# Edge streams of a four-part graph network: one-hots, scores and weights moved between VectorE, ScalarE and PSUM

## The reference

```python
score = f(table[src], dst_row[dst])          # layers 1 and 2: leaky_relu(xl[src] + xr[dst] + edge_attr @ We.T) @ att
smax  = segment_max(score, dst)
es    = exp(score - smax[dst])
alpha = es / segment_sum(es, dst)
out   = segment_sum(alpha * message[src], dst)
```

## Time and profile before

| | |
|---|---|
| median of 3 runs | 13644.97 us (13634.25 to 13649.05) |
| the profiled execution | 13576.47 us, its span 13574.4 us |
| TensorE, products | busy 10504.2 us (77%) |
| TensorE, weight loads | 8732.6 us (64%) |
| VectorE | 8519.3 us (63%), 15,786 instructions |
| ScalarE | 2406.7 us (18%) |
| GpSimd | 9220.1 us (68%) |
| DMA | 912.63 MB, mean 67 GB/s |

### The profile page before, as it was taken

One profiled execution on the slowest core, in us unless ns is written; L12 is line 12 of the kernel. 1 busy time (PEld: TensorE's weight loads), 2 busy tenths in 40 slices (PEclk: granted clock), 3 DMA queues, 4 the chain that ended last, 5 costly groups with the idle time before them and its releaser, 6 DMA issues. The chain is left out here.

```text
span 13574.4 us, 346433 instructions
## 1 busy us (share of the span) xinstructions
PE 10504.2 (77%) x102671; PEld 8732.6 (64%) x102672; DVE 8519.3 (63%) x15786; ACT 2406.7 (18%) x4954; POOL 9220.1 (68%) x8386
## 2 busy tenths in 40 slices
PE   2388888857888888488888857888888578888872
PEld 1377777746777777377777735777777357777762
DVE  7567777755777777355555544777777446666664
ACT  0011212111111122022222211111111112222220
POOL 0177777756777776577777735777777257777761
PEclk9855556555555555555555555555555555555555
DMA  0333333323333332222222223232222233333320
GB/s 16 84 75 71 73 73 73 73 42 75 72 72 73 73 71 57 39 55 54 55 54 55 54 54 106 77 78 77 77 78 72 69 96 78 78 78 78 78 64 11
DMA packets 771899, 912.63 MB, mean 67 GB/s; under 512 B 400125, under 2 KB 447616, under 8 KB 769760
## 3 DMA queue, kind: packets, MB, share of 16 engines
q0 software_dynamic: 267232, 390.16, 15.0%
q1 hardware_dynamic: 503008, 498.92, 13.0%
HBM read 791.99 MB, written 96.35 MB: 65 GB/s over the span
## 5 line engine op out<-in xcount | busy, mean ns | idle before, releaser
L914 POOL DMA_INDIRECT bs_gat<-table_b,bs_idx x1568 | 1750.7, 1117 | 506.5 <-issue 477.5
L914 POOL DMA_INDIRECT ds_gat<-table_d,ds_idx x1568 | 1749.3, 1116 | 506.7 <-issue 506.7
L914 POOL DMA_INDIRECT as_gat<-table_a,as_idx x1568 | 1740.9, 1110 | 506.6 <-issue 477.5
L914 POOL DMA_INDIRECT es_gat<-table_e,es_idx x1568 | 1725.7, 1101 | 505.6 <-issue 505.6
L914 POOL DMA_INDIRECT cs_gat<-table_c,cs_idx x1568 | 1731.0, 1104 | 491.0 <-issue 491.0
L1174 PE MATMUL ds_psM<-dstW_d,ds_hot 128*128 x9408 | 1252.7, 232 | 194.4 <-DVEq L1107 72.2
L1174 PE MATMUL es_psM<-dstW_e,es_hot 128*128 x9408 | 1253.5, 226 | 175.9 <-issue 65.3
L1174 PE MATMUL cs_psM<-dstW_c,cs_hot 128*128 x9408 | 1232.0, 183 | 182.3 <-DVEq L1100 68.9
L1174 PEld LDWEIGHTS ds_psM<-dstW_d,ds_hot 128*128 128x128 bf16 x9408 | 972.2, 103 | 481.6 <-issue 241.1
L1174 PEld LDWEIGHTS es_psM<-dstW_e,es_hot 128*128 128x128 bf16 x9408 | 962.6, 102 | 480.8 <-issue 224.4
L1174 PEld LDWEIGHTS cs_psM<-dstW_c,cs_hot 128*128 128x128 bf16 x9408 | 967.5, 103 | 473.0 <-issue 223.3
(11 more groups left out here) (758 smaller groups left out, 17937.2 us busy)
## 6 DMA issues: line engine op xcount, KB each, us to landing
as_rank<-rel_d SPq DMA_DIRECT2D x196, 256.0 KB
as_ea<-in_eaT SPq DMA_DIRECT2D x196, 256.0 KB
bs_rank<-rel_d SPq DMA_DIRECT2D x196, 256.0 KB
bs_ea<-in_eaT SPq DMA_DIRECT2D x196, 256.0 KB
cs_rank<-rel_d SPq DMA_DIRECT2D x196, 256.0 KB, 3.2
ds_rank<-rel_d SPq DMA_DIRECT2D x196, 256.0 KB, 3.3
es_rank<-rel_d SPq DMA_DIRECT2D x196, 256.0 KB, 3.4
table_e<-et_st SPq DMA_DIRECT2D x49, 544.0 KB, 2.7
```

Of the source, the lines that this page charges most:

```text
L914: g_.indirect_dma_start(gat[s][:, j, :], None, table, bass.IndirectOffsetOnAxis(ap=idxS[s][:, j:j + 1].bitcast(U32), axis=0)).then_inc(got ...
```

## The change

1. `hot` is made by ScalarE: `Square(rank - p)` into a new tile `off`, then `Relu(1 - off)`, each for two halves of 1,024 elements. Four activations stand at the end of ScalarE's step in place of two compares at the beginning of VectorE's.
2. `ahot` is laid out tile by tile. Eight `tensor_scalar` compare an iota row of 256 fp32 in a PSUM bank (`psI`) with one column of `m["rel"]` (now fp32). `psI` takes the bank of `psY`, whose parts move into `psX`.
3. In a, b, c and e `wtd` and `res` are one PSUM tile `psW`. Weigh writes it, rest subtracts in place, low reads it. Weigh waits for the low of the group before.
4. In a and b the score works in place on `psM`. ScalarE writes a fifth of the sum to `act`, VectorE waits for it and takes the maximum. `took` is given behind the reduce.
5. TensorE's transposes wait for `alphad` where they waited for `lowered`, as `psX` holds more.

```diff
-        ahot = [sb(f"ahot{s}", [P, 2 * P, GROUP], BF16) for s in range(2)]
-        mid = [sb(f"mid{s}", [P, GROUP, D]) for s in range(2)]
+        off = sb("off", [P, 2, GE], BF16)
+        ahot = [sb(f"ahot{s}", [P, GROUP, 2 * P], BF16) for s in range(2)]
...
-        psX, psY = ps("psX"), ps("psY")
+        psX, psI = ps("psX"), ps("psI")
+        if i != 3:
+            psW = ps("psW", 1024)[:, 0:GROUP * CW].rearrange("p (j c) -> p j c", c=CW)
+            wtd, res = [psW, psW], [psW, psW]
...
             def _(a):
...
+                def onehot(it, s):
+
+                    g = it * RING + s
+                    a.wait_ge(fed[s % 4], it * (3 * FEED) + (s // 4) * FEED + FEED)
+                    wait(a, made, g - 1)
+                    wait(a, hots, g)
+                    for x in range(2):
+                        a.activation(off[:, x, :], rank[s % 4][:, :], ACT.Square, bias=m["pidN"][:, x:x + 1]).then_inc(apart, 1)
+                    for x in range(2):
+                        a.wait_ge(apart, g * 2 + (x + 1))
+                        last = a.activation(hot[s % 2][:, x, :], off[:, x, :], ACT.Relu, bias=m["one"][:, 0:1], scale=-1.0)
+                    last.then_inc(hots, 1)
...
+                    if i <= 1 and within(u, GROUPS):
+                        a.wait_ge(added, u + 1)
+                        a.activation(act[s % 2][:, :, :].rearrange("p j f -> p (j f)"), psM[s % 2][:, :], ACT.Copy, scale=0.2).then_inc(fifth, 1)
...
+                    if within(u + 2, GROUPS):
+                        if known(u):
+                            onehot((u + 2) // RING, (u + 2) % RING)
+                        else:
+                            onehot(it if s + 2 < RING else it + 1, (s + 2) % RING)
...
             def _(v):
...
+                v.tensor_copy(psI[:, 0:2 * P], m["iota"][:, :]).then_inc(xch, 1)
...
-                def onehot(it, s):
-                    g = it * RING + s
-                    v.wait_ge(fed[s % 4], it * (3 * FEED) + (s // 4) * FEED + FEED)
-                    wait(v, made, g - 1)
-                    for a in range(2):
-                        last = v.tensor_scalar(hot[s % 2][:, a, :], rank[s % 4][:, :], m["pid"][:, a:a + 1], None, ALU.is_equal)
-                    last.then_inc(hots, 1)
...
                 def weigh(k, ks, kc):
                     v.wait_ge(alphad, kc + 1)
+                    if i != 3:
+                        wait(v, low, k)
...
                 def collect_hot(k, ks):
                     wait(v, summed, k * 2 - 2)
-                    v.tensor_tensor(ahot[ks % 2][:, :, :], over(m["rel"][:, bass.ds(k * GROUP, GROUP)], 1, [P, 2 * P, GROUP]),
-                                    m["rankX"][:, :, :], ALU.is_equal).then_inc(ahots, 1)
+                    for j in range(GROUP):
+                        last = v.tensor_scalar(ahot[ks % 2][:, j, :], psI[:, 0:2 * P], m["rel"][:, bass.ds(k * GROUP + j, 1)], None, ALU.is_equal)
+                    last.then_inc(ahots, 1)
...
                     if i <= 1:
-                        y = act[s % 2]
-                        link(v.tensor_tensor(x[:, :, :], dst3, gat[s][:, :, 0:D], ALU.add))
+                        link(v.tensor_tensor(dst3, dst3, gat[s][:, :, 0:D], ALU.add))
+                        v.sem_inc(added, 1)
+                        v.wait_ge(fifth, g + 1)
+                        link(v.tensor_tensor(dst3, dst3, act[s % 2][:, :, :], ALU.max))
+                        link(v.tensor_tensor(dst3, dst3, over(m["vec"][:, VECS.index(f"att{i + 1}"), :], 1, [P, GROUP, D]), ALU.mult))
+                        v.tensor_reduce(sc[s // CG][:, 0, q:q + GROUP], dst3, AX_X, ALU.add).then_inc(scored, 1)
+                        v.wait_ge(scored, g + 1)
                         v.sem_inc(took, 1)
-                        link(v.scalar_tensor_tensor(y[:, :, :], x[:, :, :], 0.2, x[:, :, :], ALU.mult, ALU.max))
-                        link(v.tensor_tensor(x[:, :, :], y[:, :, :], over(m["vec"][:, VECS.index(f"att{i + 1}"), :], 1, [P, GROUP, D]), ALU.mult))
-                        v.tensor_reduce(sc[s // CG][:, 0, q:q + GROUP], x[:, :, :], AX_X, ALU.add).then_inc(scored, 1)
...
-                                    last = pe.matmul(sums[h][a][:, bass.ds(w, 1), :], ahot[ks % 2][:, a * P:(a + 1) * P, j],
+                                    last = pe.matmul(sums[h][a][:, bass.ds(w, 1), :], ahot[ks % 2][:, j, a * P:(a + 1) * P],
...
                     if r == 0 and live:
                         pe.wait_ge(scored, xc * CG + CG)
-                        wait(pe, lowered, xc)
+                        wait(pe, alphad, xc)
```

More of the change, by code:

```diff
@@ L154, in build @@
             ident=sb("ident", [P, P]),
-            rankX=sb("rankX", [P, 2 * P, GROUP], BF16),
-            pid=sb("pid", [P, 2]),
+            iota=sb("iota", [P, 2 * P]),
+            pidN=sb("pidN", [P, 2]), one=sb("one", [P, 1]),
             vec=sb("vec", [P, len(VECS), D]),
@@ L265, in prepare @@
         LOADS = 10
-        MADE = 22
+        MADE = 23
         with nc.Block() as block:
@@ L328, in _ @@
                        allow_small_or_imprecise_dtypes=True).then_inc(made, 1)
-                g.iota(m["pid"][:, :], pattern=[[P, 2]], base=0, channel_multiplier=1,
+                g.memset(m["one"][:, :], 1.0).then_inc(made, 1)
+                g.iota(m["pidN"][:, :], pattern=[[-P, 2]], base=0, channel_multiplier=-1,
                        allow_small_or_imprecise_dtypes=True).then_inc(made, 1)
@@ L818, in stream @@
         else:
+            mid = [sb(f"mid{s}", [P, GROUP, D]) for s in range(2)]
             red = [sb(f"red{s}", [P, GROUP, 4]) for s in range(2)]
@@ L834, in stream @@
             tk1 = sb("tkO", [1, 2, P])
-        wtd = [sb(f"wtd{s}", [P, GROUP, CW]) for s in range(2)]
-        res = [sb(f"res{s}", [P, GROUP, CW]) for s in range(2)]
+        if i == 3:
+            wtd = [sb(f"wtd{s}", [P, GROUP, CW]) for s in range(2)]
+            res = [sb(f"res{s}", [P, GROUP, CW]) for s in range(2)]
         parts = [sb(f"parts{s}", [P, 3, GROUP, CW], BF16) for s in range(3)]
@@ L848, in stream @@
         masked = [sem(f"masked{s}") for s in range(3)]
-        hots, made, took, scored, sch, xch, ready, blank, wl, pch, sub, past = (
-            sem(n) for n in ("hots", "made", "took", "scored", "sch", "xch", "ready", "blank", "wl", "pch", "sub", "past"))
+        hots, made, took, scored, sch, xch, ready, blank, wl, pch, sub, past, apart, added, fifth = (
+            sem(n) for n in ("hots", "made", "took", "scored", "sch", "xch", "ready", "blank", "wl", "pch", "sub", "past", "apart", "added", "fifth"))
         turned, ended, gaveE, carried, gaveC, lowered, exped, backed, alphad = (
@@ L931, in step @@
                         a.wait_ge(backed, xc + 1)
-                        a.activation(alpha[xs][:, :, :].rearrange("p h t -> p (h t)"), psY[:, 384:384 + R], ACT.Copy).then_inc(alphad, 1)
+                        a.activation(alpha[xs][:, :, :].rearrange("p h t -> p (h t)"), psX[:, 256:256 + R], ACT.Copy).then_inc(alphad, 1)
                     if within(k, GROUPS):
@@ L941, in step @@
                         a.activation(Ex[:, :], Dx[:, :], ACT.Exp, scale=spec["scale"]).then_inc(exped, 1)
+                    if i <= 1 and within(u, GROUPS):
+                        a.wait_ge(added, u + 1)
+                        a.activation(act[s % 2][:, :, :].rearrange("p j f -> p (j f)"), psM[s % 2][:, :], ACT.Copy, scale=0.2).then_inc(fifth, 1)
                     if i == 3 and r == 3 and within(xc, CHUNKS):
                         a.wait_ge(backed, xc + 1)
-                        a.activation(alpha[xs][:, 0, :], psY[:, 384:384 + CT], ACT.Copy).then_inc(alphad, 1)
+                        a.activation(alpha[xs][:, 0, :], psX[:, 256:256 + CT], ACT.Copy).then_inc(alphad, 1)
+                    if within(u + 2, GROUPS):
[3 more added lines that the diff above has]
+                            onehot(it if s + 2 < RING else it + 1, (s + 2) % RING)
+                onehot(0, 0)
+                onehot(0, 1)
                 rounds(a, step, END)
@@ L993, in neighbours @@
                     return take.rearrange("a (x n) -> a x n", x=2)[:, :, 0:R - 1]
-                given = psY[0:1, 0:2 * (P + 1)].rearrange("a (x n) -> a x n", x=2)[:, :, 0:R - 1]
+                given = psX[0:1, P:P + 2 * (P + 1)].rearrange("a (x n) -> a x n", x=2)[:, :, 0:R - 1]
                 def highest(xc, xs, xq):
@@ L1195, in give_ends @@
                     pe.sem_inc(past, 1)
-                    pe.transpose(psY[0:1, 0:R], ends[:, 1:2], m["ident"][0:R, 0:R])
-                    pe.transpose(psY[0:1, P:P + R], ends[:, 0:1], m["ident"][0:R, 0:R]).then_inc(sem_out, 1)
+                    pe.transpose(psX[0:1, P:P + R], ends[:, 1:2], m["ident"][0:R, 0:R])
+                    pe.transpose(psX[0:1, 2 * P:2 * P + R], ends[:, 0:1], m["ident"][0:R, 0:R]).then_inc(sem_out, 1)
                 def give_carry(sem_in, value, sem_out):
@@ L1202, in give_carry @@
                     for x in range(2):
```

(4 more changed lines are left out.)

22 lines of the change are left out of this document (7 added, 15 removed).

## The result

The changed kernel takes 14,315.2 us (median; 14,307.5 to 14,316.4), the kernel before 13,647.0 us on the same chip: ratio 1.049, 95% interval 1.047 to 1.051. The forecast was 14,250 us, in a range of 13,850 to 14,900 us. The profiled execution spans 14,312.0 us, 738 us more than before's 13,574.4 us.

A forecast was written before the change was run, and what follows sets the result against it. Gathers set the pace at 11.3 us a group, TensorE next at 10.9. Layers a and b +257 us each, d +133, c and e -16 each: +615 us, about 14,190, plus 68; said 14,250 us, range 13,850 to 14,900 us.

The forecast's parts named there:

- VectorE's added work: VectorE, layers a and b: one-hots +1.23 us a group, weigh's wait +0.12, wait for ScalarE's copy +0.73, late `took` +0.81.
- reduce to flush: Score's end in a and b: `took` comes after the reduce, so 0.69 + 1.13 = 1.82 us, +0.81 us a group.
- the wait for the copy: Score in a and b: VectorE waits after the add for ScalarE's 512-element copy, 0.89 us, +0.73 us a group.
- low to weigh: VectorE, all layers but d: weigh waits for low, which breaks an overlap, +0.12 us a group (none to 0.23).
- 9.75 us a group in a without the gathers: VectorE's need in layer a before the change: 11.33 less 1.58 us waiting for gathers, its TensorE waits still included.
- Late one-hots in a, b and d: Expansion one-hots from ScalarE coming late: no term in a and b, an estimated 0.2 us a group in d.
- ScalarE's chain from flush to one-hots: ScalarE, each step: one-hot pair ready 11.1 us after the flush, leaving 1.3 us in hand before TensorE's next expansion.
- 10.93 - 0.2: TensorE's own need a group in c and e, less 0.2 us for the contiguous `ahot`; 0.47 us of lateness added, 11.20.
- Rival 3: ScalarE's chain holds TensorE in every step: +700 us, 14,950 us; decides from 0.3 us an op on; chance 0.08.
- Rival 1: Compares cheap (0.26 us each, 2.1 in all), gathers' gain kept: -160 us, 13,490 us; decides below about 0.28 us; chance 0.12.
- The rest of the span does not change: Outside the five streams: tables, merges and finishes were taken to stay as before, adding nothing to the sum.
- The 68 us between profile and median: Kernel before: median 13645.0 us against 13576.5 us profiled; this gap was added to about 14,190 us, giving 14,260 us.

## Why the prediction was right

The direction and the size came out, and part of the mechanism. The streams of a and b were forecast at 2,465 us and took 2,438 and 2,441, d's at 2,350 and took 2,370, c's and e's at 2,185 and took 2,234 and 2,245. But in a, b and d two terms of the sum were wrong, one too high and one too low. That they cancelled to 0.1 us a group was luck.

- *VectorE's added work.* Each term was close: compares 3.14 us (3.16 forecast), reduce to flush 1.81 us (1.82), the wait for the copy +0.56 us (+0.73), low to weigh +0.18 us (+0.12).
- *The base under them failed.* I took "9.75 us a group in a without the gathers" and wrote that the waits for TensorE were still in it, but did not take them out. These rows of the kernel before, waits in layer a, are what was left in:
```profile
DVE as_A L1001 <- PE as_psX L1226: 68.0, 39, 3.9
...
DVE as_carry L1018 <- PE as_psY L1203: 33.4, 35, 3.2
...
DVE as_accS L966 <- PE as_psA L1189: 27.3, 47, 1.0
```
They are 129 us, 0.66 us a group. With the terms as measured, 9.75 - 0.66 + 1.21 + 0.18 + 0.56 + 0.80 = 11.84 us (1.21 is 3.14 - 1.14 - 0.79), near the 11.81 us of the run with VectorE's one-hots. My 12.64 us were 0.83 too high. In d I had 11.85 us and that run gives 11.09. There the subtraction alone doesn't do it: the waits for TensorE in d of before are 242 us, 1.24 us a group, and 10.62 - 1.24 + 1.23 = 10.61 us is too low. Why stays open.
- *Late one-hots in a, b and d failed too.* I gave them 0, 0 and 0.2 us; they cost 0.69, 0.7 and 1.07. I had costed ScalarE's chain from flush to one-hots in an ordinary step. There it fits: in b the flushes of after stand 10.96 and 11.33 us apart, VectorE's own need of about 11. The chunk steps stand 13.42 and 13.59 us apart. In the run with VectorE's one-hots they stand 12.72 and 13.46 us apart (in layer a), 11.93 and 12.67 less the 0.79. By the rows of b what holds them is the wait of ScalarE for `added`, behind which the one-hots are queued; no usable run took out that wait alone. I costed that queue for the exponential in c and e, and did not see that the same engine order puts it behind the new copy in a and b.
- *c and e.* The late one-hots were forecast at 0.47 us a group and cost 0.46 and 0.50 (11.46 and 11.51 against 11.00 and 11.01); TensorE's wait in the chunk step is 2.13 us (1.9). The streams still got longer, since TensorE's own need is 11.0 us a group and not 10.93 - 0.2. The products did get faster (3.13 to 2.90 us in c). By how much my 10.93 was too low, and in which of TensorE's pauses, stays open.
- *Rival 3* was the truth for 0.7 to 1.1 us a group, by the chunk steps (in d, two of four steps have waits of 2.7 to 3.3 us) and not, as I priced it, by a dearer operation. Its point of decision was misplaced: ScalarE's operations are 1.04 us apart, as forecast (1.03).
- *Rival 1* was right in half: the gathers did get shorter, and eight compares that write `ahot` contiguously win 2% once they read the bf16 row and nothing waits. How much of that comes from shorter gathers and how much from faster products no run separates.
- *"The rest of the span does not change"* missed 51 us. At the end of a stream only sums are left. Their step was 4.63 us in c, with 0.64 us of it a wait for TensorE, and is 6.37 us with VectorE alone to set it. From the last score to the last sum each of the five streams now takes 11 to 12 us longer.
- The 68 us between profile and median that I carried over were before's alone; after has 1 us. In spans the forecast was +615 us against +738.

The undone parts don't price the change fully: what the score's stalls cost beside the other two costs was to be read from the two runs that fell into TensorE's pauses, and is only argued from its rows (1.36 us a group on VectorE). Shown is their price without the others, 0.4 us a group.

## What to carry to other kernels

Work that is moved to an engine with spare time goes behind that engine's waits. Follow it in the step in which those waits are longest, not in the mean step, and put it ahead of them where its inputs allow. When you estimate the need of an engine without its present bound, take out its waits for everyone (in a that came out to 0.03 us, in d it took out too much), and check that undoing one cost does not only lengthen the wait at another: here two edits gave 1.0% and 0.65% alone and 5.5% together.

## What the runs showed of the hardware

- A `tensor_scalar` compare of 256 elements with a pointer scalar starts 0.39 us after the one before when it reads fp32 from PSUM and 0.20 us after it when it reads bf16 from SBUF (eight in 3.14 and 1.63 us). The Trainium skill, "VectorE: DVE Perf Modes" (Why PSUM operands drop a tier), caps a PSUM source in fp32 at the basic rate; the slower compares from PSUM are in line with it. No run here reads fp32 from SBUF or bf16 from PSUM, so place and type of the source are not told apart.
- With the SBUF source and all else as changed a gather in a takes 986 ns on average, with the PSUM source 955, and in the kernel before, with its operation on two SBUF sources, 1,110. With that one operation replaced by the eight compares from SBUF it is 1,054.
- An activation of 1,024 bf16 elements with a pointer bias takes 1,138 ns, as the figures of "ScalarE: Activation LUTs" (What ACT_TABLE_LOAD costs) in the Trainium skill give. The next one starts after 1.04 us, and it is that which counts in a chain on one engine. The same section lets back-to-back activations overlap by about 93 ns, and the trace agrees; the prediction's 0.4 us more for the four left that out.
- In six of the twelve runs TensorE paused for 0.5 or 1.1 us between single products; these kernels, and the kernel before beside them, took over 18,100 us. One chip showed this in four runs and not in a later one. The cause is not known.
